# One layer on one core: GpSimd's 64 scatters dealt out 2, 1 or 4 to a unit, experts' turns from unit 33

## The reference

```python
s = jnp.einsum('bhtd,bhsd->bhts', q, k)
s = s - s.mean(axis=-1, keepdims=True)
mad = jnp.abs(s).mean(axis=-1, keepdims=True) + 1e-06
s = s / mad * score_gain
s = jnp.where(causal[None, None], s, -1000.0)
r = jnp.maximum(s, 0.0) ** 4
att = r / (r.sum(axis=-1, keepdims=True) + 1e-06)
y = einsum(att, v) @ W_proj + b_proj

topv, topi = jax.lax.top_k(xn @ gate_w + gate_b, 2)
probs = jax.nn.softmax(topv, axis=-1)
for e in range(8):
    z = (xn @ w1[e] + b1[e]) * (xn @ w2[e] + b2[e])
    out += weight_e * (silu(z @ wg[e] + bg[e]) @ w3[e] + b3[e])
x = x + attention(xn) + out
```

## Time and profile before

| what | us |
|---|---|
| median of 3 runs | 847.79 |
| lowest and highest of them | 844.07, 849.59 |
| the profiled execution, its own time | 841.43 |
| its span, first to last instruction | 839.4 |
| mean granted TensorE clock over the span | 0.943 of full |

### The profile page before, as it was taken

The page is one execution under the profiler, slowest core; times in us unless marked ns, Lnnn a source line. Parts: engine busy times, 40 slices in busy tenths (PEclk is TensorE's granted clock), DMA queues, the critical chain, the costliest instruction groups (busy, mean ns, idle before and its releaser), DMA issues.

```text
span 839.4 us, 17649 instructions
## 1 busy us (share of the span) xinstructions
PE 747.7 (89%) x5756; PEld 336.1 (40%) x5759; DVE 685.1 (82%) x1877; ACT 677.5 (81%) x1523; POOL 596.9 (71%) x533
## 2 busy tenths in 40 slices
PE   3969888889998999999999899999999999999884
PEld 1622121214444454444444454444444454453223
DVE  7659989899878888887877778887877978778896
ACT  4777979698888788888887688988878898878890
POOL 4007687847987787886877587797767787777874
PEclk9986888889999999999999899999999999999898
DMA  8885121273414524351423423242233515230623
GB/s 252 265 224 176 39 70 56 57 223 86 117 52 126 138 67 86 108 133 59 94 97 94 115 82 88 76 149 92 58 95 108 163 35 149 83 61 14 172 60 109
DMA packets 58348, 90.84 MB, mean 108 GB/s; under 512 B 8960, under 2 KB 41344, under 8 KB 58256
## 3 DMA queue, kind: packets, MB, share of 16 engines
q1 hardware_dynamic: 52560, 79.93, 34.2%
q0 software_dynamic: 4544, 9.38, 3.6%
q10 hardware_dynamic: 1152, 0.40, 0.2%
HBM read 61.29 MB, written 28.06 MB: 106 GB/s over the span
## 4 chain that ended last, share of the span: by engine, by line
PE 50%; DVE 20%; ACT 13%; issue 9%; POOL 4%; DMA 2%; SPq 0%; DVEq 0%; ACTq 0%; POOLq 0%
PE bank L956 20%; DVE W L1277 11%; PE bank L991 8%; PE bank L971 6%; ACT U L825 5%; PE bank L1011 5%; DVE junk_V L1269 4%; PE bank L996 3%; PE bank L1019 3%; ACT W L839 2%; PE bank L881 2%; ACT junk_A L817 2%; POOL W L665 2%; POOL W L674 1%; DVE W L1281 1%
## 5 line engine op out<-in xcount | busy, mean ns | idle before, releaser
L956 PE MATMUL bank<-W,VS 128*10 128x512 f32 (+3 forms) x1536 | 300.3, 512 | 20.8 <-ACT yq L809 9.3
L1277 DVE SCALAR_TENSOR_TENSOR W<-bank,U 128x512 f32<-128x512 f32 (+1 forms) x512 | 300.4, 649 | 22.0 <-ACT U L825 20.3
L956 PE MATMUL bank<-U,usel 128*10 128x512 f32 (+3 forms) x1536 | 296.8, 510 | 0.0
L1269 DVE TENSOR_SCALAR_CACHE_REDUCE junk_V<-bank 128x512 bf16<-128x512 f32 (+3 forms) x445 | 218.3, 533 | 70.6 <-PE bank L1011 69.6
L825 ACT ACTIVATE U<-bank 128x512 f32<-128x512 f32 (+1 forms) x512 | 253.0, 598 | 27.7 <-PE bank L1019 27.4
L674 POOL TENSOR_TENSOR W<-W 128x1024 f32<-128x1024 f32 (+2 forms) x159 | 231.2, 1459 | 46.9 <-DVE W L1277 39.0
L665 POOL TENSOR_TENSOR W<-W,causal 128x512 f32<-128x512 f32 x128 | 163.5, 1277 | 98.2 <-DVE W L1277 64.0
L839 ACT ACTIVATE W<-W 128x256 f32<-128x256 f32 (+2 forms) x225 | 191.0, 875 | 18.5 <-POOL W L665 17.9
L1019 PE MATMUL bank<-QS,KS 48*128 48x512 bf16 (+3 forms) x768 | 154.1, 336 | 22.8 <-DVE W L1277 15.8
L817 ACT ACTIVATE junk_A<-bank 128x512 bf16<-128x512 f32 (+3 forms) x195 | 88.2, 463 | 46.8 <-PE bank L1011 46.2
L1011 PE MATMUL bank<-KS,QS 48*128 48x512 bf16 (+3 forms) x640 | 101.6, 328 | 2.0 <-issue 1.3
(11 more groups left out here) (158 smaller groups left out, 668.5 us busy)
## 6 DMA issues: line engine op xcount, KB each, us to landing
wb<-in_experts SPq DMA_DIRECT2D x39, 707.0 KB, 4.6
qk_parts<-parts SPq DMA_DIRECT2D x8, 768.0 KB, 7.6
KS<-qk_parts SPq DMA_DIRECT2D x192, 32.0 KB
QS<-qk_parts SPq DMA_DIRECT2D x192, 32.0 KB
xt_all<-sorted_x SPq DMA_DIRECT2D x39, 130.0 KB, 5.2
gat<-weighted_y SPq DMA_DIRECT2D x8, 512.0 KB, 7.9
sorted_x<-xt_all SPq DMA_DIRECT2D x3, 1300.0 KB, 12.4
v_stationary<-vb SPq DMA_DIRECT2D x4, 640.0 KB, 5.3
```

Source lines behind the costliest of these rows:

```text
L956: last = pe.matmul(acc[32 * g:32 * g + VW, lo:HALF], usel[:, :] if of_u else VS[q % 2][:, j, :, g], (U if of_u else W)[n % NU][:, g, 0:HAL ...
L1269: last = vec.tensor_scalar(junk["V"][k_th % 2][:, at:at + w], piece(m)[:, at:at + w], 0.0, None, ALU.max, ALU.add, accum_out=msum[:, m // ...
L1277: vec.scalar_tensor_tensor(W[n % NU][:, g, 0:w], score(n, g), 0.0, U[n % NU][:, g, 0:w], ALU.max, ALU.mult).then_inc(w_done, 1)
```

## The change

The constant `PER_STEP` goes. A table `SCATTER_AT` deals the scatters by the kind of unit: two in a unit with a mask and 512 queries, one in a narrower unit with a mask, four in a unit without a mask, until 64 are dealt. That takes 30 units (`N_SCATTER`), and all that was counted from unit 32 is now counted from 30: GpSimd's squares, the turns (from 33 and not 35), the loads of sorted rows, the reload of x, the bias.

```diff
     SCATTERS = TOPK * NT
-    PER_STEP = 2
+    SCATTER_AT = [0]
+    while SCATTER_AT[-1] < SCATTERS:
+        at = (len(SCATTER_AT) - 1) % NS
+        SCATTER_AT.append(min(SCATTERS, SCATTER_AT[-1] + ((2 if LOW[at] == 0 else 1) if DIAG[at] else 4)))
+    N_SCATTER = len(SCATTER_AT) - 1
     POOL_SQUARES = [(1,), (1,), (1,), (1,), (0,), (0,), (0,), (0, 1), (), (1,), (1,), (1,)]
-    by_pool = lambda n, p: n * PER_STEP >= SCATTERS and p in POOL_SQUARES[n % NS]
+    by_pool = lambda n, p: n >= N_SCATTER and p in POOL_SQUARES[n % NS]
...
-    FFN_FROM, FFN_TO = SCATTERS // PER_STEP + 3, ALL - 12
+    FFN_FROM, FFN_TO = N_SCATTER + 3, ALL - 12
...
-    BIAS_FROM = SCATTERS // PER_STEP + 6
+    BIAS_FROM = N_SCATTER + 6
...
-            T_AT = [max(SCATTERS // PER_STEP + 1, STEP_OF["tx", i // 2] - 4) for i in range(NX)]
+            T_AT = [max(N_SCATTER + 1, STEP_OF["tx", i // 2] - 4) for i in range(NX)]
...
-                if n == SCATTERS // PER_STEP + 4:
+                if n == N_SCATTER + 4:
                     sp.dma_start(xr[:, :, :], x_v).then_inc(x_again, 16)
...
-                if 0 < n * PER_STEP < SCATTERS:
+                if 0 < n < N_SCATTER:
                     pool.wait_ge(w_done, 4 * n - 2)
-                for k in range(n * PER_STEP, min(SCATTERS, (n + 1) * PER_STEP)):
+                for k in range(SCATTER_AT[n], SCATTER_AT[n + 1]) if n < N_SCATTER else ():
                     scatter(k // NT, k % NT)
```

## The result

The changed kernel takes 870.53 us (median of 6 runs, 867.32 to 872.87), the kernel before 848.69 beside it (6 runs, 844.07 to 852.28): ratio 1.0256 [1.0228, 1.0285], slower by 21.8 us. The prediction was 861.8 in a range from 851 to 871: the sign held, the time lies 0.5 us inside the upper end of the range, and the size was 8.7 us short.

The account below looks back on a forecast made before the run. The prediction took TensorE to bound the experts' stage and VectorE, stopped now and then, the scatter stage. Terms of +14.0 us on the profiled 841.43 gave 855.4; moved 6.4 onto the median, 861.8 us, range 851 to 871.

Parts of the forecast that it names:

- Unit 8: Mask 8 ends 6.1 us late behind eighteen scatters, TensorE's average runs at low clock, W of unit 11 late: +7.1 us.
- Unit 12: One scatter fewer before mask 11, so mask 12 is 0.2 us late and not 1.13: -0.9 us, bounds 0 and -1.1.
- Unit 20: Open landing wait, then seventeen scatters; mask 20 ends 9.5 us late and W of unit 23 comes late: +10.4 us.
- Unit 24: Mask of unit 24 relieved in the same way as that of unit 12: -0.9 us.
- units 28 to 31: Scatters there hold up nothing; GpSimd takes squares of units 30 and 31 from ScalarE: -0.7 us, bounds 0 and -1.5.
- Turns from unit 33: 119 turns over 147 units, not 145; some 1.6 move into two units with TensorE gaps: -1.0 us, 4 either way.
- The sum: All terms from unit 8 to the turns added up: +14.0 us, which takes the profiled 841.43 us to 855.4.
- the base: Profiled execution lay 6.4 us under the timed median of 847.79; that difference was added onto the median, giving 861.8 us.
- The first rival: Relief alone: scatters in wide units cost GpSimd's queue nearly nothing, masks 8 and 20 stay covered; -3.5, 844.3 us, chance 0.08.
- The second rival: Half a stall: masks late, but averages at high clock, shorter landing, turns gain 2.5; +7.4, 855.2 us, chance 0.12.
- The third: Turns fall badly, costing 4 more, and TensorE's low clock outlives the average by 2 to 3 us; +21, 869 us, chance 0.08.

Follow-up runs that it names:

- first chip: Chip of the earliest follow-up runs, which ran the kernel before in 840.53 us (13 runs) and the deal alone in 854.29 us.
- third group: Later runs on the second chip: the kernel before unaltered 848.12 us, the changed kernel unaltered 870.22 us, the deal alone 869.90 us.
- deal alone: Scatters dealt as in the changed kernel, all else counted from unit 32 as before: 854.29 us on the first chip, 869.90 us in the third group.
- second chip: Another chip used for follow-up runs, which ran the kernel before in 851.21 us (9 runs) and later in 848.68 us (12 runs).
- the kernel with them moved: The changed kernel with only the experts' turns put back to unit 35: 868.09 us (4 runs), ratio 1.0212.

## Why the prediction was right, and where it was wrong

**Unit 8, +7.1.** Right on the first chip in every link: mask 6.2 us late (6.1 said), average at the low clock for 3.60 (3.61), W of unit 11 35.1 - 28.2 = +6.9. Where the result was measured the place was right, and that the longer row does it, but the link was another: W came late, the mask did not, and unit 11 lost 42.0 - 30.7 = 11.3 (third group, against before there).

**Unit 12, -0.9.** Unit 15 stands at 50.5 - 44.6 = +5.9 after +6.9 at unit 11: -1.0. In the third group 10.2 after 11.3: -1.1. Right on both.

**Unit 20, +10.4.** From +5.9 at unit 15 to 88.7 - 72.9 = +15.8 at unit 23: +9.9. GpSimd waited 2.76 us for the landing before the iota in the deal alone (3.05 said), and mask 20 was 8.8 late (9.5). Right. In the third group +22.7 after +10.2: +12.5.

**Unit 24, -0.9; units 28 to 31, -0.7.** +14.6 at unit 27 and +14.1 at unit 31: -1.2 and -0.5. The squares were not moved in that run; their part stays unmeasured, since the kernel with them moved and the deal alone have ratios of 1.0212 and 1.0239 on the second chip, with intervals that overlap.

**Turns from unit 33, -1.0.** Wrong in sign: +3.1, at the edge of the 4 us allowed both ways. The step that failed is that "some 1.6 turns move into two units in which TensorE has gaps". Their gaps did not take them, unit 31 to 35 became 1.25 us longer and the quad after it 1.84, and the relief that this should give to the units behind them did not show (536 us from unit 47 to 179 with either). Why the relief fails was not tried.

**The sum.** By the first chip's own parts, 13.8 for the deal and 3.1 for the turns, the whole is +16.9 us, 2.9 over the forecast of +14.0: the turns are 4.1 over theirs, the rest of the sum is 1.2 under its 15.0. The changed kernel as a whole was never run on that chip. Where it was run, in three sets of runs, it lost 18.6 to 21.8 us by the medians. What is missing goes with the late signals: the deal alone costs some 20 us on the chip that has them and 13.8 on the one that has not. That the time still fell into the range is in part luck: the second stall was not in the sum, and 0.5 us more would have left the range.

**The step that failed is the one on the base.** The prediction noted that the profiled execution lay 6.4 us under the median and 2.6 under the lowest run, and put the difference "onto the median" as if it were only an offset. It was a second regime: that trace has no late signal, the one of before on the second chip, where the median was 848.12, has. Of the 10.6 us between these two traces 8.4 have come up by the end of unit 31, among the scatters, and the change made their rows longer: the deal alone then differs by 15.1 us there.

**The first rival**, a scatter that costs the queue nothing, is out: steps of 1.26 in the row of eighteen, and with memsets of 1.30 in place of eight scatters mask 8 is 5.9 us late where it was 6.2. The Trainium skill, "DMA: Bandwidth & Descriptors", section on the anatomy of one DMA on the gpsimd path, calls descriptor generation small; the measurement decides, 0.96 us each of GpSimd's time and 0.30 to the next. The Trainium skill, "Perfetto Trace Analysis", section on DMA instructions of the SWDGE, says that the instruction's end in a profile is the end of descriptor generation, not of the movement of data; the trace agrees, with landings 2.8 to 3.0 us behind that end where GpSimd waits for them. **The second rival** (half a stall) fell with the low clock in the first chip's average. **The third** (the turns fall badly, +21) has the right time for the wrong reason: the turns gave 3.1 of the 4 it asked for, and on the first chip the low clock outlasted the average of unit 8 by some 0.5 us (granted 0.50 up to 107.0, 0.74 from 107 to 108) and that of unit 20 by some 1.4 (0.50 still from 160.6 to 162), not by 2 to 3.

## What to carry to other kernels

Before an instruction is put into a "free" unit, count its whole queue up to the next instruction that somebody waits for: here 8 x 1.27 us against 4.35 of room, one for one beyond it. GpSimd's scatters in long unbroken rows went with a delay, on two of three chips, that the queue does not explain; waits between them that cost nothing gave 0.7% here. And if a profiled execution is faster than every timed run of the same kernel, take another profile before pricing anything from it: the two may not be the same regime.

## What the hardware showed that was not expected

- **TensorE's finished work can be signalled many microseconds late while GpSimd issues indirect scatters back to back.** The largest lateness, from the profiles that have any: 1.5 us with two scatters and two memsets in turn, 1.9 with ten scatters paced, 4.0 with ten of which eight are unbroken, 8.3 and 10.1 with rows of fourteen and twelve, 13.1 to 14.6 with rows of eighteen, 14.7 to 16.0 with rows of seventeen. The last signals are let go together, 1.0 to 4.9 us after the row's last scatter ends; in the rows of seventeen some are let go before. In the second profile of the changed kernel TensorE's are late and those of ScalarE and GpSimd are not.
- **It depends on the chip, or on something that goes with it.** Four profiles on the first chip have none, though three of them have the long queue (only one a row of eighteen scatters); all seven on the second and the one on the third have them. (Of the first profiles of the two kernels, before without them and after with them, the chips are not on record.) The kernel before takes 840.5 us on the first and 848.7 to 851.2 on the others.
- **The two kinds of trace differ in one thing more.** In the nine traces with late signals 59 to 78 of TensorE's some 1,600 semaphore events are missing, over the whole span, and in the five without them 3 or 4. Those of VectorE and ScalarE have holes in the same nine and hardly one in the five. So the rival that the recording of the execution takes part in the delay is open: every run here comes with its span and granted clock, and none tells how the kernel fares without a record.
- What holds the signals back is open. The bytes moved are an unlikely candidate, as the DMA engines' share over the quad is 0.22 in the trace of after and in that of before, and a scatter's data packets take as long in traces with late signals as without (a median of 0.19 us between 79 and 92 us in all). That the writing of descriptors and TensorE's signals share a path would fit, but no run here shows it. Nor was it tried whether scatters in rows delay TensorE when it only multiplies and signals nothing.
